# Six of eight parts of each expert's second product as split passes, with GpSimd's and VectorE's small steps moved in the order by hand

## The chip, the cores and the metric

The kernel runs on one core of one Trainium2 chip. The metric is the device time of one execution in microseconds (us). The engines are TensorE (PE, its weight loads PEld), VectorE (DVE), ScalarE (ACT), GpSimd (POOL) and the queue of SyncE (SP), which only starts DMAs.

## The reference, cut to what matters

The reference adds a cross attention to x and then a mixture of 16 experts. Only the second half is touched by the change:

```
logits = xn @ router_weight.T + router_bias          # 4096 tokens, 16 experts
_, idx = top_k(logits.T, 256)                        # each expert takes its 256 best tokens
xe = xn[idx]                                         # [16, 256, 256]
h = gelu(einsum('ecd,efd->ecf', xe, fc1) + fc1_bias) # first product, F = 1024
y = einsum('ecf,edf->ecd', h, fc2) + fc2_bias        # second product, back to D = 256
out = x + scatter_add(y * gates) / gate_sums
```

Inputs, weights and output are 32-bit floats.

## The kernel before, in words

The first 875 us or so are attention and routing; then a search finds each expert's limit, and from about 946 us on the 16 experts run one after the other. All engines walk through one list of steps, `expert_plan`, made by `schedule_experts` (L243): each engine has a function for some kinds of step and skips the others. So the place of a step in the list is its place in the queue of every engine that takes part in it. Inside an expert the list is made of 24 pieces of TensorE work, with a call of `between()` (L301) behind each; `at` counts them. Points 1 to 8 follow the eight parts of the first product (`hidden`, one part f is 128 of the 1024 hidden units), points 9 to 16 the eight parts of the second product for the first 128 tokens (`expert_out`, c = 0), and points 17 to 24 the same for the other 128 tokens (c = 1). Behind point 16 and behind point 24 comes `gate`, which empties the bank.

**Split passes.** A value is split in a high part, rounded to the format fp32r, and a low part, the rest. A product is then three matmuls: high by high, high by low, low by high. The first product is always made so (L953). ScalarE writes the high part of the weights (`split`, L1178), GpSimd subtracts for the low part (L1284, recorded as w_lo<-w_raw,w_hi at L1290); of the gathered tokens ScalarE writes the high part and VectorE the low part (`turn_tokens`, L943, L1186, L1713: xe_lo). In the second product (L968) the parts f below FS are made so for experts from SPLIT_FROM = 2 on (`in_parts`, L646); the others are one plain fp32 matmul each. For a split part ScalarE also writes h_hi (L1192) and VectorE h_lo (L1727); the weights of all split parts of an expert are split in one step, `split_out`, on ScalarE (L1204) and VectorE (L1722, recorded as w_lo<-w,w_hi at L1725). FS is 4. For c = 1 the plain parts come first (`OUT_ORDER`), since their weights and hidden units need nothing more.

**The rest of an expert.** `list_hot` (two parts, VectorE), `list_count` (TensorE, 32 small matmuls), `list_join` (VectorE) and `list_spread` (TensorE, VectorE) turn slots into a list of token numbers, from the second pair on for two experts at a time (`group_of`). `gather` (L1299) and `scatter` (L1319) are indirect DMAs that GpSimd issues, two each per expert. `gate` and `scale_out` (L1733, L1741) are VectorE's and write y_out. SyncE walks through the same list (from L1855): behind `split` (e, 1) it loads the first weights of expert e + 2 (`load_w1`, L1831), which waits until both low halves of expert e exist; at `gate` (e, 1) it loads the second weights of e + 2 (`load_w2`, L1838), and `renew_rows` waits for the first three gathers.

TensorE's hidden (e, f) waits for the activation of the part four before it (four banks), for xe_lo and for the low halves of the weights. ScalarE's hidden steps come behind `split_out` of their own expert in its queue.

Of the kernel before, what the change touches and what calls it, by code (L numbers as in the profile page):

```python
# [26 lines left out]
E, F = 16, 1024  # L27
# [7 lines left out]
FT = F // P  # L35
# [195 lines left out]
FIRST_SPLITS = (6, 8, 10, 12)  # L231


SPLIT_FROM, FS = 2, 4
OUT_ORDER = (tuple(range(FT)), tuple(range(FS, FT)) + tuple(range(FS)))


def group_of(e):

    return e if e < 2 else e // 2 + 1  # L240


def schedule_experts():  # L243
    plan = []

    def add(*piece):
        plan.append(piece)

    def first_expert():

        add("order", 1)
        add("turn_tokens", 0)
        add("slots", 1)
        add("list_hot", 1, 0)
        add("list_hot", 1, 1)
        for f in range(FT):
            add("hidden", 0, f)
            if f == 4:
                add("list_count", 1)
                add("list_join", 1)  # L260
            elif f == 5:
                add("list_spread", 1)
                add("gather", 1)
                add("scale_gates")
                add("list_hot", 2, 0)
                add("list_hot", 2, 1)
                add("gather_gates", 0)
                add("gather_gates", 1)
        for c in range(2):
            for n, f in enumerate(OUT_ORDER[c]):  # L270
                add("expert_out", 0, c, f)
                if c and n == 4:
                    add("list_count", 2)
                    add("list_join", 2)
                elif c and n == 6:
                    add("list_spread", 2)
                    add("gather", 2)
                    add("gather_gates", 2)
                    add("renew_rows")
            add("gate", 0, c)  # L280
            if c == 0:
                add("turn_tokens", 1)

    for r in range(SEARCH_ROUNDS):
        add("search", r)
        if r in FIRST_SPLITS:
            add("split", *divmod(FIRST_SPLITS.index(r), 2))
    add("order", 0)
    add("slots", 0)
    for part in range(2):  # L290
        add("list_hot", 0, part)
    for piece in ("list_count", "list_join", "list_spread"):
        add(piece, 0)
    add("gather", 0)
    first_expert()
    for e in range(1, E):
        lists = group_of(e + 3) if e % 2 and e + 3 < E else None
        counts = group_of(e + 2) if e % 2 == 0 and e + 2 < E else None
        state = {"point": 0}

        def between():  # L301

            state["point"] += 1
            at = state["point"]
            if at == 2 and e == 1:
                for c in range(2):
                    add("scale_out", 0, c)
            if at == 2 and counts:
                add("list_count", counts)
            if at == 5 and counts:  # L310
                add("list_join", counts)
            if at == 7 and counts:
                add("list_spread", counts)
            if at == (9 if e == 1 else 4):
                for c in range(2):
                    add("scatter", e - 1, c)
            if at == 1 and e == 1:
                add("split", 2, 0)
            if at == 9 and e + 1 < E:
                add("split", e + 1, 1)  # L320
            if at == 13 and e + 2 < E:
                add("split", e + 2, 0)
            if at == 10 and e + 2 < E:
                add("gather", e + 2)
            if at in (9, 17) and lists:
                add("list_hot", lists, at // 17)
            if at == 3 * FT - 4 and e + 1 < E:
                add("turn_tokens", e + 1)
            if at == 3 * FT - 2 and e + 1 >= SPLIT_FROM and e + 1 < E:
                add("split_out", e + 1)  # L330

        for f in range(FT):
            add("hidden", e, f)
            between()
        for c in range(2):
            for f in OUT_ORDER[c]:
                add("expert_out", e, c, f)
                between()
            add("gate", e, c)
            if e == E - 1:  # L340
                add("scale_out", e, c)
                add("scatter", e, c)
        if e < E - 1:
            for c in range(2):
                add("scale_out", e, c)
    return plan
# [1584 lines left out]
```

How the kernel before makes its waits and increments, by code:

```python
    def wait_ge(self, sem, value):  # L115
        if value > self.reached.get(sem.name, 0):
            self.reached[sem.name] = value
            self.engine.wait_ge(sem, value)
# [609 lines left out]
        def columns():  # L728
            on.wait_ge(*misc.vacant("columns"))
            on.wait_ge(small_loaded, 16 * N_SMALL)
            on.wait_ge(*columns_made.at("mask_rows"))
            pe.transpose(misc.bank("columns")[:, 0:B * CT], mask_rows_f[:],
                         ident[0:B * CT, 0:B * CT]).then_inc(misc.fill("columns"), 1)
# [1 line left out]
        def spread(b, s, half):  # L735
            use = ("spread", b, s, half)
            src, out = spread_source(b, s), misc.bank(*use)
            on.wait_ge(*misc.vacant(*use))
            on.wait_ge(*(ctx_centred.at(b, s) if s < 2 else x_centred.at(b)))
            on.wait_ge(small_loaded, 16 * N_SMALL)
            for i in range(4):
                last = pe.transpose(out[:, i * P:(i + 1) * P], src[:, i, half * P:(half + 1) * P], ident[:])
            last.then_inc(misc.fill(*use), 1)
# [1 line left out]
        def kv(b, tile):  # L745
            use = ("kv", b, tile)
            on.wait_ge(*misc.vacant(*use))
            on.wait_ge(*weights_low.at("ctx"))
            for half in range(2):
                on.wait_ge(*z_lo_made.at(b, tile // 4, half))
# [8 lines left out]
        def qk(b, i):  # L759
            use = ("qk", b, i)
            on.wait_ge(*misc.vacant(*use))
            on.wait_ge(*weights_low.at("lat"))
            for half in range(2):
                on.wait_ge(*z_lo_made.at(b, 2, half))
```

## Time and profile before

| | us |
|---|---|
| median of 3 runs | 1182.78 (1182.5 to 1183.49) |
| the profiled execution's own time | 1185.55 |
| its span in the profile | 1183.7 |
| PE busy | 1027.0 (87%) |
| DVE busy | 785.5 (66%) |
| ACT busy | 671.8 (57%) |
| POOL busy | 797.3 (67%) |
| mean granted clock | 0.939 of full speed |

Times in the rows are us from the start of the span. A row of a timeline gives start, duration, engine, line, operation, what is written and read, how many instructions are merged (x4), and in brackets how long the engine sat idle before it and what ended that. The chain is the work that ended last, followed backwards: start, duration, what. A granted clock of 1.00 is 2.4 GHz, 0.50 is 1.2 GHz. Matmul records overlap, since they are pipelined; distances between starts tell what one costs.

### The profile page before, as it was taken

The page shows a single profiled execution, that of the slowest core. Times are in us where ns is not written, and L with a number is a line of the kernel's source. Part 1 is how long each engine was busy: PE and PEld are TensorE (multiplying, and loading weights), DVE is VectorE, ACT ScalarE, POOL GpSimd, SP SyncE. Part 2 cuts the span into 40 slices and gives each one's busy share as a digit, 9 for nine tenths or more (in the row PEclk, how much of TensorE's full clock was granted, in tenths as well). Part 3 has the DMA queues.
Part 4 walks back from the last instruction along what each step waited for, and adds up shares of the span by engine and source line. Part 5 has one row for each costly group of instructions (what it writes and reads, how often), then busy time and mean ns, then how long its engine had stood idle before and what let it go on. Part 6 is the DMA issues. An engine that isn't in the chain of part 4 may idle for free.

```text
span 1183.7 us, 17328 instructions
## 1 busy us (share of the span) xinstructions
PE 1027.0 (87%) x5982; PEld 634.1 (54%) x5982; DVE 785.5 (66%) x1811; ACT 671.8 (57%) x1300; POOL 797.3 (67%) x891
## 2 busy tenths in 40 slices
PE   3669999999999999999999999998740298999996
PEld 2535445544644654554464465443220188999995
DVE  3666767876786886777677668775038765676752
ACT  5636756676576566657657655534414235656662
POOL 3305986797699589679769958969802248777773
PEclk9859999999999999999999999999965599999998
DMA  6020010011011002001110000000017227666752
GB/s 173 5 58 1 7 35 18 1 37 42 2 55 42 2 1 73 26 1 55 42 39 1 7 20 19 1 20 19 11 41 203 80 35 234 194 193 216 224 172 27
DMA packets 73479, 71.99 MB, mean 61 GB/s; under 512 B 38608, under 2 KB 67408, under 8 KB 69296
## 3 DMA queue, kind: packets, MB, share of 16 engines
q1 hardware_dynamic: 65392, 62.08, 16.4%
q0 software_dynamic: 6336, 8.70, 4.2%
q8 instruction: 48, 0.79, 0.3%
q10 hardware_dynamic: 1664, 0.10, 0.1%
q14 instruction: 39, 0.32, 0.1%
HBM read 56.97 MB, written 13.83 MB: 60 GB/s over the span
## 4 chain that ended last, share of the span: by engine, by line
PE 72%; POOL 10%; DVE 7%; issue 5%; ACT 4%; ACTq 1%; DMA 0%; POOLq 0%; DVEq 0%
PE bank L717 55%; PE pair_bank L717 12%; POOL prob_sum L1256 8%; ACT probs L1001 2%; DVE c_in L1559 2%; PE bank L790 2%; PE bank L742 2%; DVE masked_scores L1476 1%; PE bank L870 1%; POOL z_lo L1235 1%; PE bank L949 1%; DVE maxima L1469 1%; PE bank L778 0%; ACT c_in L1001 0%; POOL gate_rows L1315 0%
## 5 line engine op out<-in xcount | busy, mean ns | idle before, releaser
L1256 POOL TENSOR_TENSOR prob_sum<-prob_sum,probs 128x256 f32<-128x256 f32 x640 | 475.6, 775 | 80.9 <-ACT probs L1001 74.4
L1001 ACT ACTIVATE probs<-bank,mask_col 128x512 f32<-128x512 f32 x256 | 162.1, 686 | 109.7 <-PE bank L717 107.8
L1476 DVE CUSTOM_DVE_ANT_0 masked_scores<-pair_bank,mask_bias 128x512 bf16<-128x512 f32 x256 | 166.4, 688 | 81.7 <-PE pair_bank L717 81.5
L717 PE MATMUL bank<-probs,v_nat 128*64 128x512 f32 x768 | 205.1, 616 | 0.4 <-ACT probs L1001 0.4
L1469 DVE TENSOR_REDUCE maxima<-pair_bank 128x2 f32<-128x1024 f32 x64 | 78.3, 1224 | 47.2 <-PE pair_bank L717 47.2
L1001 ACT ACTIVATE probs<-bank 128x512 f32<-128x512 f32 x128 | 69.5, 594 | 66.0 <-PE bank L717 65.9
L717 PE MATMUL pair_bank<-k_hi,q_hi 64*128 64x512 f32 x384 | 93.2, 479 | 13.7 <-DVE maxima L1476 9.1
L717 PE MATMUL bank<-q_hi,k_hi 64*128 64x512 f32 x384 | 94.2, 484 | 10.7 <-ACT probs L1001 8.8
L1256 POOL TENSOR_TENSOR prob_sum<-probs 128x256 f32<-128x256 f32 x64 | 44.8, 731 | 82.1 <-ACT probs L1001 70.4
L1506 DVE RECIPROCAL bank<-bank 128x128 f32<-128x128 f32 x64 | 58.6, 944 | 58.4 <-PE bank L717 58.4
L717 PEld LDWEIGHTS bank<-q_hi,k_hi 64*128 64x128 f32 x384 | 37.2, 184 | 106.5 <-ACT probs L1001 55.3
L1325 POOL DMA_INDIRECT out_x<-y_out,token_index x32 | 54.7, 1709 | 39.1 <-DVE y_out L1749 34.2
L717 PE MATMUL bank<-q_lo,k_hi 64*128 64x512 f32 x384 | 77.7, 394 | 0.0
L717 PE MATMUL bank<-q_hi,k_lo 64*128 64x512 f32 x384 | 77.4, 392 | 0.0
L717 PE MATMUL bank<-shift,one_rows 64*128 64x512 f32 x384 | 77.3, 392 | 0.0
L717 PEld LDWEIGHTS pair_bank<-k_hi,q_hi 64*128 64x128 f32 x384 | 37.8, 191 | 69.5 <-issue 27.5
L1290 POOL TENSOR_TENSOR w_lo<-w_raw,w_hi 128x1024 fp32r<-128x1024 f32 x28 | 70.0, 2500 | 7.0 <-ACT w_hi L1001 6.7
L717 PEld LDWEIGHTS bank<-probs,v_nat 128*64 128x64 f32 x768 | 38.8, 135 | 65.0 <-issue 62.8
L1235 POOL TENSOR_TENSOR z_lo<-z_full,z_hi 128x512 fp32r<-128x512 f32 x32 | 41.1, 1285 | 46.1 <-ACT z_hi L1001 46.1
L1371 DVE TENSOR_REDUCE sq_sum<-squares 128x4 f32<-128x256 f32 (+1 forms) x96 | 47.2, 496 | 25.3 <-ACT squares L1001 25.3
L1001 ACT ACTIVATE h_full<-bank,b_cols 128x256 f32<-128x256 f32 x96 | 44.0, 468 | 34.0 <-PE bank L717 33.8
L717 PE MATMUL bank<-xe_hi,w_hi 128*128 128x256 f32 x192 | 57.6, 300 | 5.0 <-POOL w_lo L1290 3.6
(235 smaller groups left out, 2490.7 us busy)
## 6 DMA issues: line engine op xcount, KB each, us to landing
w_raw<-in_fc SPq DMA_DIRECT2D x16, 1024.0 KB, 4.8
w<-in_fc SPq DMA_DIRECT2D x16, 1024.0 KB, 6.3
c_in<-in_ctx SPq DMA_DIRECT2D x16, 384.0 KB, 3.4
x_in<-in_x SPq DMA_DIRECT2D x8, 512.0 KB, 4.9
out_x<-x_in SPq DMA_DIRECT2D x8, 512.0 KB, 3.5
rows_scratch<-xr_nat SPq DMA_DIRECT2D x8, 512.0 KB, 3.5
c_in<-in_ctx SPq DMA_DIRECT2D x16, 128.0 KB, 3.5
b_rows<-in_fc_bias SPq DMA_DIRECT2D x16, 128.0 KB, 5.6
```

The source lines that it names most:

```text
L717: return pe.matmul(out, lhsT, rhs, start=start, stop=stop, skip_group_check=True)
L742: last = pe.transpose(out[:, i * P:(i + 1) * P], src[:, i, half * P:(half + 1) * P], ident[:])
L790: last = pe.transpose(misc.bank(*use)[:, j * P:(j + 1) * P], k, ident[:])
L1001: return act.activation(out, a, f, bias=bias, scale=scale)
L1235: tt(to[place][rows, half, :], z_full[rows, half, :], as32(z_hi[place][rows, half, :]), ALU.subtract).then_inc(z_lo_made.sem, 1)
L1256: last = tt(total[:, half], first[:, half], p[:, half], ALU.add)
L1290: tt(w1_lo[i][:, n, :], w1_raw[i][:, n, :], as32(w1_hi[i][:, n, :]), ALU.subtract).then_inc(w_lo_made.sem, 1)
L1325: pool.indirect_dma_start(out_rows, bass.IndirectOffsetOnAxis(ap=tokens_of(e, c), axis=0), y_out[i][:, c, :], None, compute_op=ALU.add).th ...
L1371: dve.tensor_reduce(sq_sum[:, place:place + heads], squares[square_turn[use] % 2][:, 0:heads * DH].rearrange("p (h d) -> p h d", d=DH), AX ...
L1469: last = dve.tensor_reduce(maxima[:, :, j, g], pair_bank[:], AX, ALU.max)
L1476: last = dve.tensor_tensor_reduce(masked_scores[:, hh, :], pair_bank[:, hh, :], mask_bias[:, 512 * g:512 * (g + 1)], 1.0, MASKED, ALU.add, ...
L1506: state["inverse"] = step.of(dve.reciprocal(sums, sums))
```

## The change

FS goes from 4 to 6, so two more parts of the second product of each of the 14 experts from 2 on are split, and the four tiles w2_hi, w2_lo, h_hi and h_lo (two buffers each) are larger by half. The c = 1 order becomes 6, 7, 0 to 5, for the first two experts too. In `between()` steps move:

- `split` (2, 1) from point 9 to point 3 of expert 1; other `split` (e + 1, 1) stay at 9; `split` (e + 2, 0) from 13 to 12.
- `scatter` of expert 0 from point 9 to 10 of expert 1; others stay at 4.
- `gather` (e + 2) at point 10 becomes `gather` (e + 1) at point 1, from expert 2 on. So it now stands ahead of the scatters.
- `list_hot`, second part: from point 17 of an odd expert to point 9 of the even expert behind it; `list_count` and `list_join` from points 2 and 5 to 18; `list_spread` from 7 to 21.

```
-SPLIT_FROM, FS = 2, 4
+SPLIT_FROM, FS = 2, 6
...
-            if at == 2 and counts:
-                add("list_count", counts)
-            if at == 5 and counts:
-                add("list_join", counts)
-            if at == 7 and counts:
-                add("list_spread", counts)
-            if at == (9 if e == 1 else 4):
+            if at == 1 and e == 1:
+                add("split", 2, 0)
+            if at == (3 if e == 1 else 9) and e + 1 < E:
+                add("split", e + 1, 1)
+            if at == (10 if e == 1 else 4):
                 for c in range(2):
                     add("scatter", e - 1, c)
-            if at == 1 and e == 1:
-                add("split", 2, 0)
-            if at == 9 and e + 1 < E:
-                add("split", e + 1, 1)
-            if at == 13 and e + 2 < E:
+            if at == 12 and e + 2 < E:
                 add("split", e + 2, 0)
-            if at == 10 and e + 2 < E:
-                add("gather", e + 2)
-            if at in (9, 17) and lists:
-                add("list_hot", lists, at // 17)
+            if at == 9 and lists:
+                add("list_hot", lists, 0)
+            if at == 9 and counts:
+                add("list_hot", counts, 1)
+            if at == 18 and counts:
+                add("list_count", counts)
+                add("list_join", counts)
+            if at == 1 and 2 <= e < E - 1:
+                add("gather", e + 1)
             if at == 3 * FT - 4 and e + 1 < E:
                 add("turn_tokens", e + 1)
+            if at == 3 * FT - 3 and counts:
+                add("list_spread", counts)
             if at == 3 * FT - 2 and e + 1 >= SPLIT_FROM and e + 1 < E:
                 add("split_out", e + 1)
```

`lists` is set for odd experts, `counts` for even ones. FT is 8.

## Rows read from the trace of the kernel before

**Rows 1.** The page: its head, and the granted clock in 40 slices.
```profile
span 1183.7 us, 17328 instructions
...
PEclk9859999999999999999999999999965599999998
```

**Rows 2.** One stretch: length, busy us of PE, PEld, DVE, ACT, POOL, clock, DMA.
```profile
1020.00:1040.00 20.00, 20.00 (x141) 18.69 (x141) 12.26 (x17) 12.17 (x21) 15.68 (x11) 1.00 0.61 178
```

**Rows 3.** The chain that ended last, experts 6 and 7: start, us, what.
```profile
1039.30 3.61 PE bank L717 x50
...
1053.73 2.38 PE bank L717 x18
...
1062.84 1.73 PE pair_bank L717 x8
1065.00 1.43 PE pair_bank L717 x12
1066.43 3.61 PE bank L717 x50
```

**Rows 4.** Waits of PE, 940 to 985 us: in total, times, longest.
```profile
PE bank L717 <- POOL w_lo L1290: 3.6, 1, 3.6
```

**Rows 5.** The chain around the start of expert 2.
```profile
974.97 2.36 POOL w_lo L1290
...
981.02 2.38 POOL w_lo L1290
...
983.54 5.11 PE bank L717 x50
...
992.74 3.15 PE bank L717 x20
```

**Rows 6.** One stretch in expert 2, columns as in rows 2.
```profile
985.00:986.00 1.00, 1.00 (x8) 0.78 (x7) 0.92 (x3) 0.60 (x3) 0.70 (x2) 0.50 0.94 336
```

**Rows 7.** Timeline of POOL, experts 6 and 7.
```profile
1051.05 1.01 POOL L1308 DMA_INDIRECT gathered<-rows_scratch,token_index  x1 [0.16 <-issue]
...
1053.37 2.40 POOL L1290 TENSOR_TENSOR w_lo<-w_raw,w_hi 128x1024 fp32r<-128x1024 f32 x1
...
1061.22 2.81 POOL L1290 TENSOR_TENSOR w_lo<-w_raw,w_hi 128x1024 fp32r<-128x1024 f32 x1
```

**Rows 8.** Timeline of SP's queue: second weights of expert 2, first weights of expert 4.
```profile
974.83 2.30 SPq L1843 DMA_DIRECT2D w<-in_fc  x1
...
983.48 0.33 SPq L1836 DMA_DIRECT2D w_raw<-in_fc  x1
```

**Rows 9.** Timeline of ACT: split of second weights; steps in expert 7.
```profile
982.24 1.06 ACT L1001 ACTIVATE w_hi<-w 128x1024 fp32r<-128x1024 f32 x1 [3.40 <-DMA w<-in_fc]
...
1054.73 0.48 ACT L1001 ACTIVATE h_full<-bank,b_cols 128x256 f32<-128x256 f32 x1 [0.84 <-PE bank L717]
...
1055.56 0.46 ACT L1001 ACTIVATE h_full<-bank,b_cols 128x256 f32<-128x256 f32 x1
...
1060.09 2.00 ACT L1001 ACTIVATE w_hi<-w_raw 128x1024 fp32r<-128x1024 f32 x2
```

**Rows 10.** Timeline of DVE, experts 1 to 7.
```profile
978.87 0.69 DVE L1719 TENSOR_TENSOR xe_lo<-bank,xe_hi 128x512 fp32r<-128x512 f32 x1
983.33 1.23 DVE L1725 TENSOR_TENSOR w_lo<-w,w_hi 128x1024 fp32r<-128x1024 f32 x1 [3.77 <-ACT w_hi L1001]
...
1052.97 0.69 DVE L1719 TENSOR_TENSOR xe_lo<-bank,xe_hi 128x512 fp32r<-128x512 f32 x1 [2.37 <-ACT xe_hi L1001]
1053.92 2.94 DVE L1725 TENSOR_TENSOR w_lo<-w,w_hi 128x1024 fp32r<-128x1024 f32 x1 [0.26 <-ACT w_hi L1001]
...
1057.64 1.42 DVE L1731 TENSOR_TENSOR h_lo<-h_full,h_hi 128x256 fp32r<-128x256 f32 x4
...
1062.93 0.43 DVE L1739 TENSOR_TENSOR y_out<-bank,b_rows 128x256 f32<-128x256 f32 x1 [1.60 <-issue]
```

**Rows 11.** From issue to landing of the gathers of rows.
```profile
DMA to landing us min/median/max: 2.8/5.0/6.1
```

## The prediction, made blind

> **What bounds the kernel now.** I read the page first: 1183.7 us of span, and a granted clock that dips twice, in the search (slices 31, 32) and slightly in slice 34 [rows 1]. Attention and search hold none of the changed steps, so only what follows 946 us counts. The table of stretches comes next. From 1000 to 1160 us all of its rows look like [rows 2]: TensorE busy for the whole stretch at full clock, GpSimd for 15.7 of 20, the others for 12. There the kernel ends as early as TensorE's own list of work allows. The chain says the same and gives the period: expert 6 (with its list) runs from 1039.30 to 1053.73 = 14.43, expert 7 (no list) to 1066.43 = 12.70 [rows 3], and the pairs behind it look the same. Only one spot behind 960 us is different: TensorE waits 3.6 us for the low half of expert 2's first weights [rows 4]. The chain shows why: GpSimd makes one half (974.97), issues expert 0's two scatters, and only then makes the second (981.02 to 983.40) [rows 5]. After this pause TensorE ran at a granted 0.50, 1.2 GHz, for a while [rows 6], which made expert 2's start 5.11 us long where expert 6 takes 3.61 for the same 50 matmuls: 1.5 us more [rows 3, 5].
>
> **The change part by part.** The sums are against the profiled execution (1185.55, span 1183.7); the median of the runs is 2.8 us below it, and I take the difference over to it as it is.
>
> *A. Two more split parts.* In expert 7 four plain parts take 1.73 us and four split ones 1.43 [rows 3], so one part saves (1.73 - 1.43) / 4 = 0.075 us. Two parts, two token halves and 14 experts make 56: **-4.2 us**, all on TensorE's path. I take this, as the row measures exactly the two forms. The Trainium skill, "FP8 and Floating Point Precision", section "TensorE Precision Notes", counts four passes through the array for true FP32. Read as four against three that would be 0.43 / 4 = 0.108 a part and -6.1 us; the trace has 1.43 / 1.73 = 0.83 and not 0.75, so it speaks against that.
>
> What the other engines do more must hide:
> - ScalarE: two more h_hi. A part with h_hi comes every 0.83 us (1054.73 to 1055.56) [rows 9], against 0.71 of TensorE; it falls back by 0.12 a part. With six, h_hi (5) is ready at S + 1.0 + 6 x 0.83 = S + 6.0, where S is the start of the expert on TensorE; it is first used behind S + 5.7 + 5 x 0.36 = S + 7.5. The step w2_hi grows from 1.06 to some 1.6, ends about S + 0.7, and h_full (0) is due at S + 1.0. Hidden.
> - VectorE: w2_lo grows from 1.1 to 1.65. It took 1.23 in one place and 2.94 in another [rows 10]; in the second GpSimd's subtraction ran from 1053.37 to 1055.77 [rows 7] and VectorE's ended 1.09 behind that. So a subtraction of two SBUF tiles stands still while GpSimd makes its own. At worst, behind a GpSimd step that ends at S + 2.4: w2_lo to S + 4.1, gate and scales (1.0) to S + 5.1, h_lo (0) at S + 5.5, needed at S + 5.7. Hidden even then, with little to spare; without that cover each expert would lose what is missing.
>
> *B. GpSimd's order.* Its queue in an expert becomes gather, scatter, split, split: two gathers 2.3 (1051.05 to 1053.37) [rows 7], two scatters 3.7 (977.33 to 981.02) [rows 5], two splits of 2.4; with gaps about 11.3, in 12.4. ScalarE's two w_hi start 6.4 behind S in expert 7 (1060.09) [rows 9] and 0.8 later with two more h_hi: the first is there at S + 8.2, so GpSimd splits from S + 8.3 to 10.7 and 10.8 to 13.2. With an odd expert now 12.4 long, that ends at S' + 0.8 of the next, about where ScalarE has w2_hi ready. VectorE then has w2_lo at S' + 2.5 instead of 3.1, and all of h_lo by the end of the first product. The first low half is needed at S' and is there 1.7 earlier. The gathers now start at S' + 0.9 or so and land after 5.0, at worst 6.1 [rows 11], by S' + 8.5; TensorE turns the tokens at S' + 10.3. The scatters follow them when VectorE has scaled. list_hot moves under GpSimd's DMA issues and can push a split back by 0.5. Steady state: 0.
>
> *C. The start of expert 2.* The second half no longer stands behind the scatters: it runs 977.5 to 979.85, and xe_lo is ready at 979.56 [rows 10]; TensorE goes on at 979.9, not at 983.54. But then other things are late. Expert 2's second weights were asked for at 974.83 [rows 8], held up by the wait for early gathers, and ScalarE could split them only at 982.24 [rows 9], which is untouched; load_w1 (4) moves from 983.48 [rows 8] to 979.9 and shares the DMA engines with them, so I take up to 2 us more. ScalarE's h_full (0) is behind w2_hi: 982.24 + 1.6 = 983.8 to 985.8. TensorE makes four parts and waits. GpSimd has issued the scatters by 983.5 and makes the half for expert 3 until 985.9; VectorE's w2_lo stands behind it: 987.5; gate and scales 988.5, h_lo (0) 988.9. The second product starts at about 989.3 instead of 992.74 [rows 5], 3.4 earlier; of this 1.7 comes back, since list steps that stood inside expert 2's first product (14.43 - 12.70) [rows 3] now stand in its second. **-1.7 us**. Bounds: -5.1 (stall and clock loss both go) and 0 (weights land 2 us later still, or the clock falls again). I take the value from the chain of dates.
>
> *D. The list steps on TensorE.* 32 matmuls and the spread stay as many. xe_lo ends at 1053.66, TensorE starts at 1053.73 [rows 3, 10]: each boundary waits for it. In six experts list_spread (some 0.3) now stands in that wait. Between 0 and -0.3 x 6; I take **-0.5**. A new wait: TensorE's spread at point 21 wants list_join, 0.5 us of VectorE behind the count at 18, and 1.5 us of work lie between. Behind it wait only the last three parts. If that cover went, some tenths in six experts.
>
> The tail (last matmul, gate, scale, scatter) stays. The sum: -4.2 - 1.7 - 0.5 = -6.4, and 1182.8 - 6.4 = **1176.4 us**.
>
> **The rivals.** A measurement of this kernel can tell some 0.2% (2.4 us) from no change.
>
> *R1, the early gain is eaten.* Expert 2 becomes bound by its second weights, and what GpSimd gave up comes back as waits for w2_hi and w2_lo. For it: the row of 974.83 and the shared DMA. Then A and D alone: 1182.8 - 4.5 = 1178.3.
>
> *R2, all of the pause goes.* w2_lo gets in front of GpSimd's step at 983.4, a near tie by the dates above, and the clock holds: -4.2 - 5.1 - 0.5 gives 1173.0. Against it: the weights' date.
>
> *R3, slower.* One mechanism: GpSimd's second split now lies over xe_lo of the next expert, from S' - 1.6 to S' + 0.8, where before it began behind it (1053.37 against 1052.97) [rows 7, 10]. If xe_lo stood still for it as w2_lo does, it would end at S' + 1.5 instead of S' - 0.1: 1.6 us at each of the seven boundaries behind an expert without a list, +11, so 1187.6. It decides from 0.9 us a boundary on (7 x 0.9 = 6.4). Against it: VectorE's gate reads a bank and one SBUF tile, as xe_lo does, and at 1062.93, in the middle of GpSimd's step, took 0.43 [rows 7, 10], no longer than elsewhere. The Trainium skill, "SBUF — State Buffer", section "Who interferes with whom", says that a VectorE instruction with at most one SBUF input, outside the two-port modes, doesn't contend with GpSimd; by that rule R3 doesn't happen, and the trace agrees with the 0.43.
>
> *R4, no change.* The saving per part is lost to h_lo or the h_hi pace: within 2 us of 1182.8. For it: the margin of 0.2 in the worst order. Against: that order is just the one the moves take away.
>
> **How the numbers follow.** The forecast 0.48, R1 0.22, R2 0.12: faster 0.86 with a remainder for mixed cases of the same sign (0.04). R4 0.06. R3 0.08. Range: low end 1172.5, just under R2; high end 1180.5, R1 with another 2 us of small waits in it. That leaves R3, R4 and a little below out.
>
> **What would show it.** Right: a pair of experts at 27.13 - 8 x 0.075 - 0.1 = 26.4 in the chain; the 3.6 wait for w_lo gone, and instead TensorE waits near 983 to 986 for h_full and near 988 for h_lo; w_lo<-w,w_hi at 1.6 to 1.8 with no 2.9 or 3.4; xe_lo still 0.69 under GpSimd's step; expert 3 starts near 997.5 (999.47 before, less 2.0). Wrong: xe_lo over 1 us (R3); expert 3 before 995 (R2) or at 999 (R1); h_lo as the releaser of TensorE in the steady part; a clock under 1.00 behind 1000 us; or a pair far from 26.4.

## The result, and the profile after

The change makes the kernel slower: 1192.7 us median of four runs (1190.16 to 1194.85) against 1182.64, ratio 1.0083 with a 95% interval from 1.0063 to 1.0104. The forecast was 1176.4, 1172.5 to 1180.5. The profiled execution is the fastest of the four (1190.16, span 1188.3, against 1185.55 and 1183.7 before). So the medians are 10.1 us apart and the two profiled spans only 4.6: the one before was taken of an execution 2.9 above its median, the one after of one 2.5 below its own. The traces account for the 4.6; how the remaining 5.5 divide is not shown.

The page after, its head and the granted clock, answer to [rows 1]; below them, from the table of stretches, two stretches that answer to [rows 2] (length, busy us of PE, PEld, DVE, ACT, POOL, clock, DMA).

```profile
span 1188.3 us, 17496 instructions
...
PEclk9869999999999999999999999999865599999998
```

```profile
1020.00:1040.00 20.00, 17.89 (x141) 17.25 (x140) 15.02 (x21) 12.62 (x24) 17.08 (x9) 1.00 0.63 190
...
1080.00:1100.00 20.00, 19.99 (x146) 19.55 (x147) 13.67 (x26) 13.12 (x27) 15.66 (x8) 0.91 0.66 202
```

TensorE, which was busy for all of each stretch before, now has gaps in what was its steady state, and in one of these two stretches a lower clock instead. The waits of PE behind 940 us name the gap (waiting line, releaser: us in total, times, longest); [rows 4] had one line of this size, for w_lo.

```profile
PE bank L718 <- DVE list L1695: 8.8, 5, 2.1
PE bank L718 <- POOL w_lo L1291: 1.9, 2, 1.0
...
PE bank L718 <- DVE h_lo L1732: 1.2, 1, 1.2
PE bank L718 <- ACT h_full L1002: 1.1, 1, 1.1
```

The chain that ended last, experts 2 to 15, answers to [rows 3, 5]. The lines of 1009.19, 1037.68, 1065.75, 1153.01 and 1165.41 start experts 4, 6, 8, 14 and 15; the last is TensorE's last piece.

```profile
1009.19 2.37 PE bank L718 x18
...
1037.68 2.38 PE bank L718 x18
...
1047.50 1.05 PE bank L718 x32
1048.82 3.07 DVE list L1695
1052.34 1.25 PE pair_bank L718 x9
...
1065.75 2.38 PE bank L718 x18
...
1081.85 3.48 PE bank L718 x18
...
1153.01 2.39 PE bank L718 x18
...
1165.41 2.38 PE bank L718 x18
...
1174.37 3.03 PE pair_bank L718 x22
```

In the timeline of PE expert 3 starts at 996.00:

```profile
996.00 0.36 PE L718 MATMUL bank<-xe_hi,w_hi 128*128 128x256 f32 x1 [1.04 <-POOL w_lo L1291]
```

The whole difference of the two spans follows from these dates. The experts begin 1.9 us earlier (the token transposes of expert 0 at 942.76 instead of 944.65). That lies ahead of every changed step, and in the ten traces below the same piece starts anywhere from 942.45 to 944.97, so I take it as scatter. Expert 3 starts 3.5 earlier, so the start of expert 2 gained 1.6. Expert 4 starts 3.0 earlier; 0.5 is lost again, in a wait for w_lo. From expert 4 to 14 the chain takes 1153.01 - 1009.19 = 143.8 instead of 1147.82 - 1012.17 = 135.65: **8.2 us lost in five pairs**. Experts 14 and 15 take 24.4 instead of 25.0, 0.6 gained. Sum: -1.9 - 1.1 + 8.2 - 0.6 = +4.6, which is 1188.3 - 1183.7. The 8.2 are in turn 8.8 of waits for the list and 2.9 of two falls of the granted clock (18 matmuls in 3.48 us at 1081.85 and in 3.65 at 1139.35, instead of 2.14), less some 3.5 that five shorter pairs give back.

A pair is now 1065.75 - 1037.68 = 28.07, where 27.13 was before and 26.4 forecast. Its odd expert (12.3) is as forecast; the even one, with the list, is long. The chain passes through a step of VectorE, list, that takes 3.07 us. The timelines of DVE and of POOL for that expert show why (start, duration, engine, line, what, idle time before):

```profile
1048.57 0.21 DVE L1693 TENSOR_TENSOR list_parts<-bank,own_block 32x64 f32<-32x64 f32 x1 [1.47 <-PE bank L718]
1048.82 3.06 DVE L1695 SCALAR_TENSOR_TENSOR list<-list_parts 32x32 f32<-32x32 f32 x1
1051.81 0.67 DVE L1720 TENSOR_TENSOR xe_lo<-bank,xe_hi 128x512 fp32r<-128x512 f32 x1
1052.41 0.20 DVE L1703 TENSOR_TENSOR picked<-pick,bank 128x64 f32<-128x64 f32 x1
...
1052.97 1.75 DVE L1726 TENSOR_TENSOR w_lo<-w,w_hi 128x1536 fp32r<-128x1536 f32 x1
```

```profile
1044.62 2.49 POOL L1326 DMA_INDIRECT out_x<-y_out,token_index  x1 [0.31 <-issue]
1046.58 5.25 POOL L1291 TENSOR_TENSOR w_lo<-w_raw,w_hi 128x1024 fp32r<-128x1024 f32 x2
1053.34 2.27 POOL L1309 DMA_INDIRECT gathered<-rows_scratch,token_index  x1 [1.51 <-DVE token_index L1711]
```

list_join is two VectorE steps, and the second waits for the first. The first reads a bank and one SBUF tile and takes 0.21 in the middle of GpSimd's pair of splits. The second reads two slices of an SBUF tile, 32 by 32 elements; it took 0.18 in other places, and here ends at 1051.88, when GpSimd's pair ends at 1051.83. TensorE's spread waits for it (the chain goes on at 1052), and xe_lo, itself not slowed (0.67), stands behind it in VectorE's queue.

### The profile page after: what moved, and what is told of

It reads as the page before. It is cut to its first block, busy times and chain, and to the rows that moved or that the text cites. A ratio compares the mean times of both kernels' runs of the same rounds, so it can differ in the third digit from the quotient of the medians.

```text
span 1188.3 us, 17496 instructions
## 1 busy us (share of the span) xinstructions
PE 1021.8 (86%) x6038; PEld 633.2 (53%) x6038; DVE 798.6 (67%) x1839; ACT 683.9 (58%) x1328; POOL 817.0 (69%) x891
## 4 chain that ended last, share of the span: by engine, by line
PE 68%; POOL 11%; DVE 8%; issue 5%; ACT 4%; DMA 1%; ACTq 1%; POOLq 0%; DVEq 0%
PE bank L718 53%; PE pair_bank L718 10%; POOL prob_sum L1257 8%; ACT probs L1002 2%; DVE c_in L1560 2%; PE bank L791 2%; PE bank L743 2%; DVE list L1695 1%; POOL w_lo L1291 1%; DMA out_x<-y_out,token_index 1%; POOL z_lo L1236 1%; POOL out_x L1326 1%; DVE masked_scores L1477 1%; PE bank L871 1%; ACT c_in L1002 1%
## 5 line engine op out<-in xcount | busy, mean ns | idle before, releaser
L1309 POOL DMA_INDIRECT gathered<-rows_scratch,token_index x32 | 50.0, 1563 | 39.6 <-DVE token_index L1711 33.3
L1291 POOL TENSOR_TENSOR w_lo<-w_raw,w_hi 128x1024 fp32r<-128x1024 f32 x28 | 73.7, 2796 | 4.7 <-ACT w_hi L1002 4.7
```

Source lines behind the costliest of these rows:

```text
L1291: tt(w1_lo[i][:, n, :], w1_raw[i][:, n, :], as32(w1_hi[i][:, n, :]), ALU.subtract).then_inc(w_lo_made.sem, 1)
L1309: pool.indirect_dma_start(gathered[i][:, c, :], None, rows_dram, bass.IndirectOffsetOnAxis(ap=tokens_of(e, c), axis=0)).then_inc(gather_do ...
```

## The experiments

T1 names that step: held off by GpSimd's two splits in a row, it is late, with everything queued behind it. T2: the larger w2_lo and the additional h_lo and h_hi are late. T3: GpSimd's order makes TensorE wait for w_lo by itself. T4: the late place of the list steps costs by itself, whatever they read. Ratios are to the kernel before on the same chip; the four runs of the first group share their runs of before, so do the four of the second and the two of the third.

**1. The moves alone.**
```
-SPLIT_FROM, FS = 2, 6
+SPLIT_FROM, FS = 2, 4
```


> The changed kernel with FS = 4: the moves alone. Theory T1 (list_join's second step has two SBUF inputs and stands still behind GpSimd's two splits in a row, xe_lo queues behind it, TensorE waits some 1.7 us in six experts): the waits stay, DVE's list step is near 3 us, and the kernel is slower than the changed one by about the 4.2 us of the split passes, near 1196. Rival T2 (the larger split_out and the two more h_lo and h_hi are what is late): the waits go and the time is at or under 1181.

Measured: 1184.5 against 1185.2, ratio 0.9993 (0.9974 to 1.0011). T1 as I had put it was wrong here by 11 us, for the waits are gone but for one; T2 had the waits right, though not its time. But the step shows T1's mechanism with another overlap. Timeline of POOL, then of DVE, expert 6, which starts at 1038.36:

```profile
1045.85 4.67 POOL L1291 TENSOR_TENSOR w_lo<-w_raw,w_hi 128x1024 fp32r<-128x1024 f32 x2 [1.22 <-ACT w_hi L1002]
```

```profile
1049.65 0.91 DVE L1695 SCALAR_TENSOR_TENSOR list<-list_parts 32x32 f32<-32x32 f32 x1
```

The pair ends at 1050.52 and the step at 1050.56. With FS = 4 the pair lies 1.3 us earlier (1050.52 against 1051.83, in an expert that starts 0.7 later: 2.0 us), and holds the step for 0.7 instead of 2.9, which the 1.5 us of work between count and spread can hide. So the moves are not slow by themselves; with six parts GpSimd's pair lies later and holds the step for longer than the cover.

**2. Six parts in the old order.**
```
-SPLIT_FROM, FS = 2, 4
+SPLIT_FROM, FS = 2, 6
```
(in the kernel before.)

> The kernel before with FS = 6 and nothing moved. T1: the 56 passes save 0.075 us each and nothing new waits, 1178.5 with 1176.5 to 1180; w_lo<-w,w_hi in the worst order at 3.5 to 4 us. T2: slower than 1182.6, with TensorE waiting for h_lo or w_lo in most experts.

Measured: 1207.6, ratio 1.0181 (1.0146 to 1.0216). Both theories as written miss: T1's number by 29 us, and T2 had the side right but not the place, since most of the waiting is for xe_lo. So six parts in the old order are slower than the changed kernel, and the moves win back about 1%. The waits of PE:

```profile
PE bank L717 <- DVE xe_lo L1719: 13.2, 5, 2.7
PE bank L717 <- DVE list L1694: 3.8, 6, 0.9
PE bank L717 <- POOL w_lo L1290: 3.3, 1, 3.3
```

and the timelines of DVE and POOL at the end of an odd expert:

```profile
1040.60 3.79 DVE L1678 TENSOR_SCALAR hot_ids<-hot_lo,token_in_tile 128x1024 bf16<-128x1024 bf16 x1
1044.31 1.21 DVE L1679 TENSOR_TENSOR hot_ids<-hot_lo,tile_ids 128x1024 bf16<-128x1024 bf16 x1
1045.45 0.68 DVE L1719 TENSOR_TENSOR xe_lo<-bank,xe_hi 128x512 fp32r<-128x512 f32 x1
```

```profile
1041.14 2.96 POOL L1290 TENSOR_TENSOR w_lo<-w_raw,w_hi 128x1024 fp32r<-128x1024 f32 x1
```

The waits for xe_lo are T1 with another victim. list_hot's second part stood at point 17; its first step takes 0.49 alone and here ends 0.3 behind GpSimd's split (1044.10), then the second step and xe_lo follow. Its trace rows name one data tile and a second small operand, so it isn't only subtractions of two large tiles that are held. The same steps in the timeline of DVE of the kernel before:

```profile
1063.27 1.05 DVE L1678 TENSOR_SCALAR hot_ids<-hot_lo,token_in_tile 128x1024 bf16<-128x1024 bf16 x1
1064.24 1.21 DVE L1679 TENSOR_TENSOR hot_ids<-hot_lo,tile_ids 128x1024 bf16<-128x1024 bf16 x1
1065.67 0.69 DVE L1719 TENSOR_TENSOR xe_lo<-bank,xe_hi 128x512 fp32r<-128x512 f32 x1 [0.21 <-ACT xe_hi L1001]
```

There VectorE still sat idle for 0.21 us ahead of xe_lo; with the splits later and the expert shorter the steps are on the path, in five experts. Two smaller terms are not T1 itself. The chain through expert 6:

```profile
1046.18 5.02 PE bank L717 x50
...
1053.81 0.43 DVE h_lo L1731
```

Behind the wait the granted clock fell: the 50 matmuls take 5.02 us instead of 3.61, and so in four of the experts with a list (5.02 to 6.29). And the wait for the list stands behind h_lo in this chain, which is T2's mechanism (3.8 us in six experts).

**3. The list steps back at their old points**, all else as changed.
```
+            if at in (9, 17) and lists:
+                add("list_hot", lists, at // 17)
+            if at == 2 and counts:
+                add("list_count", counts)
+            if at == 5 and counts:
+                add("list_join", counts)
+            if at == 7 and counts:
+                add("list_spread", counts)
```
(and the new places taken out.)

> The changed kernel with list_hot, list_count, list_join and list_spread back at their points of before; gathers, scatters and splits stay moved. T1: the five waits for the list step go, a pair of experts takes 26.5 us and the time is 1176 to 1179. T2: as the changed kernel, 1190 or more. A second rival, T3 (GpSimd's two splits in a row are late by themselves, TensorE waits for w_lo): waits for POOL w_lo grow, 1182 or more.

Measured: 1205.7, ratio 1.0173 (1.0148 to 1.0197). My expectation of 1176 to 1179 was far off. The waits of PE:

```profile
PE bank L717 <- DVE xe_lo L1719: 16.2, 6, 3.5
PE bank L717 <- DVE list L1694: 5.2, 6, 2.2
```

and the timelines of DVE and POOL, in the same place as in run 2:

```profile
1041.53 3.41 DVE L1679 TENSOR_TENSOR hot_ids<-hot_lo,tile_ids 128x1024 bf16<-128x1024 bf16 x1
```

```profile
1038.12 5.73 POOL L1290 TENSOR_TENSOR w_lo<-w_raw,w_hi 128x1024 fp32r<-128x1024 f32 x2 [0.66 <-ACT w_hi L1001]
```

The waits are those of run 2 again: list_hot's two steps now stand behind the whole pair of splits, which ends at 1043.85; the second, 1.21 alone, ends at 1044.94. The clock fell here too, behind three of these waits (50 matmuls in 4.92 to 5.13 us). T3 falls: TensorE has no wait for w_lo left.

**4. list_join in one step.**
```
-            settle(tt(parts ... ALU.mult))
-            stt(list16[...], parts[:, :, 1, :], float(P), parts[:, :, 0, :], ALU.mult, ALU.add).then_inc(joined.sem, 1)
+            tt(parts, list_bank ..., own_block ..., ALU.mult).then_inc(joined.sem, 1)
...
-            mm(list_bank[:, 64:64 + 16 * n], expand16[0:16 * n, :], list16 ..., True, True)
+            for a in range(2):
+                last = mm(list_bank[:, 64:64 + 16 * n], expand16[0:16 * n, :], list_parts[0:16 * n, a, 0:n, :] ..., a == 0, a == 1)
...
-        pool.tensor_copy(tile_ids[:], tile_ids_f[:])
+        pool.tensor_scalar(tile_ids[:], tile_ids_f[:], float(P), None, ALU.mult)
```


> The changed kernel, but list_join is one VectorE step that reads a bank and one SBUF tile; its second step, the one with two SBUF inputs, is replaced by a second small matmul that adds in the bank (tile numbers are made 128 times as large). Same places in the order. T1: that step took 3 us only because GpSimd held it off; the waits go, a pair takes 26.6 us, 1176 to 1180. Rival T4 (the late place of the list steps costs by itself, whatever the operands): the waits for the list stay at 1 us or more and the time is over 1187.

Measured: 1180.8, ratio 0.9961 (0.9947 to 0.9975), faster than both kernels. No wait for the list is left, and in the chain a pair is 1062.34 - 1035.78 = 26.56:

```profile
1035.78 2.39 PE bank L718 x18
...
1062.34 2.39 PE bank L718 x18
```

GpSimd's pair is where it was (8.9 to 14.2 us behind the start of the expert, in both kernels); only the step that it could hold is gone. T4 falls: the place costs nothing that shows.

**5. GpSimd's second split waits for list_join.**
```
             on.wait_ge(*w_hi_made.at(e, n))
+            if n == 0 and e >= 4 and e % 2 == 0:
+                on.wait_ge(*joined.at(group_of(e)))
```


> The changed kernel, and GpSimd's second split of each even expert waits until list_join is done; nothing else. T1 (GpSimd's pair holds list_join's second step off, and xe_lo behind it): that step falls from 3.1 us to under 1 (the first split can still cover its start), TensorE's waits for the list shrink from 8.8 us in sum to under 3, and the time is 1180 to 1185 though GpSimd starts that split later. T4 (the late place of the list steps costs by itself): no gain, or slower by GpSimd's delay.

Measured: 1180.6 against 1186.3, ratio 0.9943 (0.9922 to 0.9963). With the step left as it is and one wait more in the program, the time falls by 1.3% against the changed kernel. Timelines of DVE and POOL, expert 6, and the chain over one pair:

```profile
1050.95 0.78 DVE L1697 SCALAR_TENSOR_TENSOR list<-list_parts 32x32 f32<-32x32 f32 x1
```

```profile
1048.74 2.93 POOL L1293 TENSOR_TENSOR w_lo<-w_raw,w_hi 128x1024 fp32r<-128x1024 f32 x1
1051.86 2.40 POOL L1293 TENSOR_TENSOR w_lo<-w_raw,w_hi 128x1024 fp32r<-128x1024 f32 x1 [0.19 <-issue]
```

```profile
1039.81 2.38 PE bank L718 x18
...
1066.13 2.39 PE bank L718 x18
```

The step now stands still for the first split alone, until 1051.67, and the pair takes 26.32. It is no full cure: in expert 2 the first split alone still stretched the step to 3.64 us (chain, at 993.04), and TensorE waited 2.3 for it.

**6. Seven parts**, with list_join in one step (FS = 7).

> The kernel with list_join in one step, and FS = 7. If the split passes are paid on TensorE's path alone, 28 more parts at 0.075 us give 2 us less than with six, some 1178.5. If VectorE's and ScalarE's extra steps (w2_lo at 2.0 us, seven h_hi at 0.83 us) have used up what hid them, it is 1181 or more, with waits for h_lo or for xe_lo behind GpSimd's pair, which starts another 0.4 us later.

Measured: 1182.7, ratio 0.9966 (0.9947 to 0.9984): nothing gained over six. The waits of PE have xe_lo again (2.9 us, five times), a pair takes 26.81 (1037.93 to 1064.74), and the chain has a step of list_hot in front of xe_lo, 3.33 us where it takes 1.22 alone:

```profile
1033.50 3.33 DVE hot_lo L1689
1036.86 0.03 DVE y_out L1740
1037.20 0.69 DVE xe_lo L1720
1037.93 2.40 PE bank L718 x18
```

**7. The changed kernel again.**

> The changed kernel once more, on the chip of the others and with another profile. T1: slower than before by 0.6 to 1.1%, five or six waits for the list step, and a spread between executions of 4 us or more, because in some of the waits TensorE's granted clock falls to 1.2 GHz behind them and in some not (1.4 us each).

Measured: 1195.6 (1191.96 to 1200.38), ratio 1.0077 (1.0051 to 1.0103), list waits 8.4 us in five places. In this execution the clock fell in experts 5 and 11 (18 matmuls in 3.65 and 3.56 instead of 2.14), in the first profile in experts 9 and 13; each time behind a wait of about 1.7 us for the list, and not behind the other three. That each such fall costs 1.3 to 1.5 us is measured. My expectation laid the spread between executions on the number of these falls, and that is not shown. The mean granted clock goes roughly with the time (the slowest of these six, 1200.38, has the lowest, 0.930), but the kernel before spreads as much without any such wait: 1184.24 to 1192.28 on the same chip, with 0.943 and 0.933.

**8. Four parts, list_join in one step.**

> The kernel with list_join in one step, and FS = 4: the moves without anything waiting. Against it FS = 6 with the same step (0.9961 of before) shows what the 56 split parts are worth when nothing waits: by the rows of before 4.2 us, so this one is near 0.9995 of before. If the saving is partly eaten it is nearer to 0.997.

Measured: 1186.0, ratio 0.9985 (0.9969 to 1.0). Against run 4 that is 0.0024, 2.8 us for the 56 parts, with intervals of 1.5 thousandths on either side, so 4.2 isn't excluded. The chain is sharper: a pair takes 1067.85 - 1040.72 = 27.13 here and 26.56 in run 4, so 0.57 for the eight parts of a pair, 0.071 each.

**9. Both mendings.**

> list_join in one step and GpSimd's second split of an even expert behind it, FS = 6. T1: each alone already took the list wait away (0.9961 and 0.9943 of before), so the two don't add: 0.994 to 0.996, a pair of experts near 26.5 us, since the extra small matmul stays. If something else of GpSimd's pair still costs (xe_lo, w2_lo), it is under 0.993.

Measured: 1181.5, ratio 0.9964 (0.9948 to 0.9980), a pair of 1061.40 - 1034.85 = 26.55. They don't add, as T1 says.

**10. The list steps back, and GpSimd's second split of an odd expert behind list_hot.**
```
             on.wait_ge(*w_hi_made.at(e, n))
+            if n == 0 and 3 <= e < E and e % 2 and e + 1 < E:
+                on.wait_ge(*ids_made.at(group_of(e + 1)))
```
(in the kernel of run 3.)

> The kernel with the list steps back at their old points (1.0173 of before, list_hot's second part 3 to 5 us behind GpSimd's pair of splits and xe_lo behind that), and GpSimd's second split of an odd expert waits until list_hot's second part is done. T1: the same mechanism made that kernel slow, so most of xe_lo's 16 us of waits go and it comes to 1.000 to 1.007 of before; what is left is the first split, which still lies over the step. Rival: the list steps inside the first product, behind six h_lo in VectorE's queue, are what costs; then it stays above 1.012.

Measured: 1.0032 (1.0012 to 1.0052), against 1.0173 without the wait. The wait of PE for xe_lo falls from 16.2 to 4.0 us:

```profile
PE bank L717 <- DVE xe_lo L1721: 4.0, 6, 0.8
```

So the same hold, on list_hot, made most of run 3's loss, and of run 2's by its rows; no clock under 1.00 is left behind 1000 us either. The h_lo ahead of list_join (five in the trace) are part of the rest: TensorE still stands for 0.6 us ahead of the spread (at 1048.08).

## Why the prediction was wrong

It failed in one step, the new wait of part D, and in its price. It said: "TensorE's spread at point 21 wants list_join, 0.5 us of VectorE behind the count at 18 ... If that cover went, some tenths". list_join took 3.3 us in all, not 0.5, and TensorE waited 1.7 to 2.1 us for it in each of five experts, 8.8 in sum. Two falls of the clock behind these waits, 2.9 us, had no term at all. What was needed to see this was in the text. Part A had read from the 2.94 us of w2_lo that a subtraction of two SBUF tiles stands still while GpSimd subtracts, and part B had dated GpSimd's pair from S + 8.3 to S + 13.2; list_join falls at S + 11 (1048.8 - 1037.7). I had weighed this hold on w2_lo and xe_lo, the large steps, and not on the small ones beside them, as if a step of 0.18 us could only be late by tenths. The trace before even had a small step held: hot_ids, 1.05 us instead of 0.49 at 1063.27 (shown in run 2). Being held costs what is left of the holder's work, not what the held step takes.

- **A, the split parts.** Right. Run 1 and run 5 have the same order, but for GpSimd's one wait, and no wait of TensorE in the pair compared: 1065.28 - 1038.36 = 26.92 for a pair with four parts, 26.32 with six. The difference, 0.60, is 8 x 0.075. Read as four passes against three it would have been 0.86. Run 4's pair, 26.56, is 0.24 longer than run 5's; the second small matmul accounts for it (0.56 against 0.33 in the chain).
- **B, what the other engines hide.** The sizes were right: w2_lo at 1.75 to 1.9 in the steady pairs (but 3.53 and 3.99 in experts 2 and 4, where none over 1.8 was expected), six h_hi in time, no steady waits for h_lo. "Steady state: 0" was wrong, through the above. Also, GpSimd's queue was longer than the 11.3 us in the sum, because gathers were put at 2.3 for two and took 2.3 + 1.0 when VectorE's w2_lo lay over the first; the pair of an even expert ended at S + 14.15, not S + 13.2.
- **C, the start of expert 2.** The size was near, 1.6 gained against 2.0 forecast for the start of expert 3, in part by luck. The dates named came: w2_hi bound by its load, TensorE waiting 1.1 for h_full and 1.2 for h_lo. VectorE's w2_lo stood still for GpSimd's step there (3.53 us). With the 1.9 of the earlier begin taken off, the second product began 0.9 sooner than forecast, and a wait of 1.0 for w_lo that had no place in the prediction (at 996.00) took that back; another 0.5 was given back one expert later. Both come from GpSimd's scatters, which waited 2.7 us for the landing of earlier ones.
- **D, the cover of xe_lo.** Half right: 27.13 before and 26.92 in run 1, 0.2 in a pair, where 0.3 at most was said.
- **R3, slower.** Its price (1.6 us a boundary) and its side were near what came, and its mechanism was wrong: xe_lo under GpSimd's pair took 0.67 to 0.69. That its 1.6 resembles the 1.7 measured is chance. The Trainium skill's rule ("SBUF — State Buffer", "Who interferes with whom") that a VectorE instruction with at most one SBUF input, outside the two-port modes, doesn't contend with GpSimd agrees with the trace for xe_lo. The same section calls the shared ports an exclusive lock; the rows showed it to me for one instruction, and I should have gone through VectorE's whole queue with it.
- **Slips.** R1's sum should be -4.2 - 0.5 = -4.7 and 1178.1, not 1178.3. The clock row of [rows 1] dips in slices 30 to 32 and shows nothing in slice 34; the fall in expert 2 stands in [rows 6] alone. Neither changes the forecast.

Much of the gain that was forecast is there once the hold is avoided: runs 5, 4 and 9 stand at 0.9943, 0.9961 and 0.9964, so 6.7, 4.6 and 4.3 us below before, with 6.4 forecast. Their intervals overlap, and only that of run 5 takes in the 6.4.

## What to carry to other kernels

When one engine's steps can hold another's, list every instruction of the held engine between the two steps on the path, the smallest too. In this case subtractions of two SBUF tiles were held, and so were a tensor_scalar (hot_ids) and a cast that read a single SBUF tile beside at most a small operand; steps that read a bank (xe_lo, the gates, the first step of list_join) were not. The price of each is what is left of the holder's steps, back to back, and all that is queued behind pays it again. A step that is over "0.2 us before it is due" is a cliff: in run 2 two more parts, which put GpSimd's splits later, turned a forecast gain into 21 us lost, falls of the clock included. The cheap cures are to feed the small step from a bank, or to make the holder wait for it.

## What was not expected of the hardware

- A VectorE step of 32 x 32 elements took 3.06 us instead of 0.18, beside GpSimd subtractions; a cast of 128 x 4 numbers with a single SBUF input took 3.46 instead of 0.17 in expert 2 (timeline of DVE of the changed kernel):

```profile
994.77 3.46 DVE L1711 CAST token_index<-list_f 128x4 uint32<-128x4 f32 x1
```

- It works in the other direction too: GpSimd's issue of a gather took 2.27 to 2.36 us instead of 1.0 when VectorE's w2_lo (two SBUF inputs) ran over it, as at 1053.34 above.
- TensorE's granted clock fell to a mean of 0.91 over 20 us (1080 to 1100), behind one wait of about 1.7 us, and stayed at 1.00 behind another of the same length (1051.9). What decides between the two is not shown.
